# Attention and feed-forward layers on one core: where the split weights of a head group are kept and read in the first batch

## The reference, cut to what matters

```python
x = x + _L0_xattn_ref(4, 256, 256, w, u, _layernorm(x), ctx_2048)      # a recurrence over time
x = x + _L0_ffn_ref(_layernorm(x), kernel, bias)                       # an 8-bit feed-forward layer
x = x + _L1_xattn_ref(_layernorm(x), ctx_2048, ...)                    # attention: nearly all of the time
x = x + _L1_ffn_ref(_layernorm(x), ...)                                # a short linear-attention layer

def _L1_xattn_ref(hidden_states, cond, ...):        # 4 batches of 256 tokens of 256 channels
    q  = _ln(_fp8_linear_pertensor(ln_out, wq, wq_scale, q_in_scale)...)    # 16 heads of 128
    k  = _ln(_fp8_linear_pertensor(ln_out, wk, wk_scale, k_in_scale)...)    # 8 groups, 2 heads each
    v  = _fp8_linear_pertensor(ln_out, wv, wv_scale, v_in_scale)
    core = _gqa(q, k, v)
    qx = _ln(_fp8_linear_pertensor(ln_out, wqx, wqx_scale, qx_in_scale)...)
    kx, vx = split(einsum('bsi,oi->bso', cond, w_kv_x)); kx = _ln(kx)
    xout = _gqa(qx, kx, vx)
    catq = _div_clamp_fp8(concatenate([core, xout]), proj_smooth)
    return einsum('bsi,oi->bso', catq, wproj) * (proj_in_scale * proj_w_scale)
```

## Time and profile before

| | before |
|---|---|
| time, median of 3 runs | 708.38 us (707.12 to 709.31) |
| span of the profiled execution, first to last instruction | 708.0 us |
| PE busy | 623.2 us (88%) |
| DVE busy | 552.2 us (78%) |
| ACT busy | 421.1 us (59%) |
| POOL busy | 274.9 us (39%) |
| DMA, mean over the span | 113 GB/s, 80.09 MB |
| mean granted TensorE clock | 0.973 of full speed |

### The profile page before, as it was taken

One profiled execution on the slowest core, in us unless ns is written; L12 is line 12 of the kernel. 1 busy time (PEld: TensorE's weight loads), 2 busy tenths in 40 slices (PEclk: granted clock), 3 DMA queues, 4 the chain that ended last, 5 costly groups with the idle time before them and its releaser, 6 DMA issues.

```text
span 708.0 us, 13489 instructions
## 1 busy us (share of the span) xinstructions
PE 623.2 (88%) x4521; PEld 496.4 (70%) x4567; DVE 552.2 (78%) x1340; ACT 421.1 (59%) x1371; POOL 274.9 (39%) x371
## 2 busy tenths in 40 slices
PE   4347989988889999999999999999899999999946
PEld 3246767766668777777777877777788787786725
DVE  7997778976677857879788669888864677769698
ACT  4246766755677736566856556657665566673631
POOL 3224663442423563433335544333333256341131
PEclk9987999998999999999999999999999999999987
DMA  8255844743472222322234223422343233320001
GB/s 268 68 181 171 305 127 143 221 156 121 110 229 111 97 98 97 98 98 98 98 112 97 98 82 109 101 97 98 98 146 108 67 124 103 98 31 1 0 1 59
DMA packets 38414, 80.09 MB, mean 113 GB/s; under 512 B 3502, under 2 KB 28746, under 8 KB 33610
## 3 DMA queue, kind: packets, MB, share of 16 engines
q1 hardware_dynamic: 38160, 79.21, 35.5%
q10 hardware_dynamic: 186, 0.02, 0.0%
HBM read 66.62 MB, written 12.60 MB: 112 GB/s over the span
## 4 chain that ended last, share of the span: by engine, by line
PE 57%; DVE 27%; issue 5%; ACT 5%; POOL 3%; DMA 2%; SPq 0%; DVEq 0%; ACTq 0%; POOLq 0%
PE bank L588 12%; PE bank L712 12%; PE bank L692 9%; PE bank L595 6%; PE bank L661 4%; PE bank L736 3%; PE bank L678 2%; DVE Cb L1755 2%; DVE nm L1740 2%; POOL rs L1318 2%; PE bank L693 1%; PE bank L726 1%; DMA WH<-wh_split 1%; DVE Cb L1770 1%; DVE Cb L1771 1%
## 5 line engine op out<-in xcount | busy, mean ns | idle before, releaser
L712 PEld LDWEIGHTS bank<-V,Pt 128*128 128x128 f32 x1024 | 126.7, 192 | 39.3 <-DVE Cb L1755 26.8
L712 PE MATMUL bank<-V,Pt 128*128 128x129 f32 x1024 | 138.0, 278 | 10.5 <-DVE Cb L1755 8.9
L1066 ACT ACTIVATE square<-bank 128x128 bf16<-128x128 f32 x372 | 98.1, 276 | 74.8 <-PE bank L588 45.3
L692 PE MATMUL bank<-QT,KTt 128*128 128x512 f32 x256 | 132.7, 600 | 2.7 <-POOL diag L1342 2.4
L1049 ACT ACTIVATE Pt<-bank 128x512 f32<-128x512 f32 x128 | 76.6, 599 | 74.6 <-remote 49.4
L1740 DVE TENSOR_REDUCE nm<-bank 128x2 f32<-128x512 f32 x128 | 82.1, 683 | 35.8 <-PE bank L678 35.7
L1318 POOL TENSOR_TENSOR rs<-ve,mhalf 128x6 f32<-128x6 f32 x64 | 94.7, 1480 | 5.3
L1342 POOL TENSOR_TENSOR diag<-identb,nm 128x512 bf16<-128x512 bf16 x64 | 67.0, 1047 | 67.3 <-DVE nm L1740 67.2
L588 PE MATMUL bank<-WQ,xq 128*128 128x256 f32 x496 | 79.0, 304 | 9.5 <-DMA WH<-wh_split 3.4
L588 PEld LDWEIGHTS bank<-WQ,xq 128*128 128x128 f32 x496 | 67.0, 196 | 21.9 <-DVE nm L1740 12.0
L1755 DVE SCALAR_TENSOR_TENSOR Cb<-bank,ro,ism 128x128 bf16<-128x128 f32 x256 | 78.1, 347 | 4.5
(11 more groups left out here) (241 smaller groups left out, 1117.2 us busy)
## 6 DMA issues: line engine op xcount, KB each, us to landing
WQ<-wq_split SPq DMA_DIRECT2D x29, 1024.0 KB, 7.7
WH<-wh_split SPq DMA_DIRECT2D x29, 384.0 KB, 8.9
ism<-smooth_inverse SPq DMA_DIRECT2D x32, 256.0 KB, 6.4
wq_split<-stage SPq DMA_DIRECT2D x6, 1024.0 KB, 4.6
wst<-in_L_xattn_wproj SPq DMA_DIRECT2D x16, 256.0 KB, 3.8
wh_split<-stageh SPq DMA_DIRECT2D x6, 384.0 KB, 4.4
wst<-in_L_xattn_wq SPq DMA_DIRECT2D x8, 256.0 KB, 4.7
wst<-in_L_xattn_wqx SPq DMA_DIRECT2D x8, 256.0 KB, 4.7
```

What stands on the lines that cost most here:

```text
L692: nc.tensor.matmul(o[:], KTt[u % 2][:, x, t * P:(t + 1) * P], QT[u % 2][:, x, :], start=True, stop=False)
L712: last = nc.tensor.matmul(o[:, h * (P + 2):h * (P + 2) + P + 1], Pt[:, x, k, h * S + t * P:h * S + (t + 1) * P], V[u % 2][:, x, k, 0:P + 1 ...
L1066: last = A(square[:, t, h], head(t, h), ACT.Square, accum_out=ss[:, t, h:h + 1])
```

## The change

`stage` and `stageh` go. `WQ` and `WH` become rings of three buffers each, and group or unit `n` uses buffer `n % 3` for making, storing, loading and reading alike. The memory in bytes stays the same, since the two stage tiles had the size of one buffer.

- In batch 0 every unit reads its weights where they were made. `load_weights` is called for `u >= 8` only, 24 times. `weights_ready(u)` for `u < 8` waits for `wl_ready`, `wr_ready` and `wc_evac`.
- Making group `g >= 3` waits, on ACT ahead of its first write, until group `g - 3` is stored and unit `g - 3` has been projected. DVE's and POOL's own waits for stores go.
- Loads run three units ahead: `load_weights(8)` and `load_weights(9)` are both issued in loop 6, then `load_weights(u + 3)` in loop `u`. The wait of each, `qkv_done >= 4 * (u' - 2)` for load `u'`, is reached at the same point of loop `u` as that of `load_weights(u + 2)` was.

```diff
-        WQ = [eb(f"WQ{i}", [P, 2, KT, 4 * P], F32R) for i in range(2)]
-        WH = [eb(f"WH{i}", [P, 3, KT, 2 * P], BF16) for i in range(2)]
+        WQ = [eb(f"WQ{i}", [P, 2, KT, 4 * P], F32R) for i in range(RING)]
+        WH = [eb(f"WH{i}", [P, 3, KT, 2 * P], BF16) for i in range(RING)]
-        stage = eb("stage", [P, 2, KT, 4 * P], F32R)
-        stageh = eb("stageh", [P, 3, KT, 2 * P], BF16)
...
-            return (stage, stageh) if u == G - 1 else (WQ[u % 2], WH[u % 2])
+            return WQ[u % RING], WH[u % RING]
+        def stored_before(g):
+            return 32 * (g // RING)
+        def loads_before(u):
+            return 32 * ((u - G) // RING + 1)
...
             def load_weights(u):
-                g = u % G
-                sp.wait_ge(s["qkv_done"], 4 * (u - 1))
-                if u < G:
-                    sp.wait_ge(s["wq01_stored"], 64)
-                    sp.wait_ge(s["wq_stored"], 16 * (g - 1))
-                    sp.wait_ge(s["wh_stored"], 16 * (g - 1))
-                else:
-                    sp.wait_ge(s["wq_stored"], 16 * (G - 2))
-                    sp.wait_ge(s["wh_stored"], 16 * (G - 2))
+                g, i = u % G, u % RING
+                if u == G:
+                    for k in range(RING):
+                        sp.wait_ge(s[f"ring{k}_stored"], 32 * len(range(k, G, RING)))
+                sp.wait_ge(s["qkv_done"], 4 * (u - RING + 1))
...
                 if u == 0:
-                    load_weights(2)
                     store_thin(3)
-                    load_weights(3)
                     store_wide(4)
-                elif u != 1 and u + 2 != G - 1 and u + 2 < UNITS:
-                    load_weights(u + 2)
+                if u == G - 2:
+                    load_weights(G)
+                if u >= G - 2 and u + RING < UNITS:
+                    load_weights(u + RING)
...
             def weights_ready(u):
-                if u < 2 or u == G - 1:
+                if u < G:
                     pe.wait_ge(s["wl_ready"], 3 * (u + 1))
                     pe.wait_ge(s["wr_ready"], u + 1)
+                    pe.wait_ge(s["wc_evac"], u + 1)
                 else:
-                    pe.wait_ge(s[f"wq{u % 2}_loaded"], 32 * (u // 2 - (u % 2 if u >= G else 0)))
-                if u < G:
-                    pe.wait_ge(s["wc_evac"], u + 1)
+                    pe.wait_ge(s[f"ring{u % RING}_loaded"], loads_before(u))
...
             def weights(g, n, o=XB):                 # on ACT
-                    if g >= 3 and n in (0, 2):
-                        act.wait_ge(s["wh_stored" if n else "wq_stored"], 16 * (g - 2))
+                    if g >= RING and n == 0:
+                        act.wait_ge(s[f"ring{g % RING}_stored"], stored_before(g))
+                        act.wait_ge(s["qkv_done"], 4 * (g - RING + 1))
...
             def narrow_parts(g):                     # on POOL
-                if g >= 3:
-                    pool.wait_ge(s["wh_stored"], 16 * (g - 2))
...
             def low_weights(g, n, o=XB):             # on DVE
-                    if g >= 3 and n == 0:
-                        dve.wait_ge(s["wq_stored"], 16 * (g - 2))
```

More of the change, by code:

```diff
@@ L70, in build_program @@
     T8 = B * NT
+    RING = 3
     main = ExitStack()
@@ L241, in round_of @@
             return (ROUNDS[u][i],) if u < G else ()
-        def halves_of(g):
-            return (WQ[g], WH[g]) if g < 2 else (stage, stageh)
         def unit_weights(u):
-            return (stage, stageh) if u == G - 1 else (WQ[u % 2], WH[u % 2])
+            return WQ[u % RING], WH[u % RING]
[3 more added lines that the diff above has]
+            return 32 * ((u - G) // RING + 1)
         def out_weights(g):
@@ L280, in build_program @@
             "x_loaded x_rest_loaded ctx_loaded rows_loaded vecs_loaded kern_loaded bias_loaded smooth_loaded wst0_loaded "
-            "wst1_loaded wp0_loaded wp1_loaded ism0_loaded ism1_loaded w3_loaded wo_loaded rw_loaded smooth_stored wq_stored wh_stored wq01_stored "
-            "wq0_loaded wq1_loaded out_stored "
+            "wst1_loaded wp0_loaded wp1_loaded ism0_loaded ism1_loaded w3_loaded wo_loaded rw_loaded smooth_stored ring0_stored ring1_stored "
+            "ring2_stored ring0_loaded ring1_loaded ring2_loaded out_stored "
             "consts_ready rowsT_done vec_ready inv_ready insw_ready smooth_inverted kernT_done kscale_ready kdiag_ready "
@@ L353, in store_wide @@
                 sp.wait_ge(s["wl_ready"], 3 * (g + 1))
-                sp.dma_start(wq_dram[g], halves_of(g)[0][:].bitcast(F32).rearrange("p a k c -> p (a k c)")
-                             ).then_inc(s["wq_stored" if g >= 2 else "wq01_stored"], 16)
+                sp.dma_start(wq_dram[g], unit_weights(g)[0][:].bitcast(F32).rearrange("p a k c -> p (a k c)")
+                             ).then_inc(s[f"ring{g % RING}_stored"], 16)
             def store_thin(g):
                 sp.wait_ge(s["wr_ready"], g + 1)
-                sp.dma_start(wh_dram[g], halves_of(g)[1][:].rearrange("p a k c -> p (a k c)")
-                             ).then_inc(s["wh_stored" if g >= 2 else "wq01_stored"], 16)
+                sp.dma_start(wh_dram[g], unit_weights(g)[1][:].rearrange("p a k c -> p (a k c)")
+                             ).then_inc(s[f"ring{g % RING}_stored"], 16)
             def load_smooth(u):
@@ L371, in load_weights @@
             def load_weights(u):
-                g = u % G
-                sp.wait_ge(s["qkv_done"], 4 * (u - 1))
-                if u < G:
-                    sp.wait_ge(s["wq01_stored"], 64)
-                    sp.wait_ge(s["wq_stored"], 16 * (g - 1))
-                    sp.wait_ge(s["wh_stored"], 16 * (g - 1))
-                else:
-                    sp.wait_ge(s["wq_stored"], 16 * (G - 2))
-                    sp.wait_ge(s["wh_stored"], 16 * (G - 2))
-                sp.dma_start(WQ[u % 2][:].bitcast(F32).rearrange("p a k c -> p (a k c)"), wq_dram[g]
-                             ).then_inc(s[f"wq{u % 2}_loaded"], 16)
-                sp.dma_start(WH[u % 2][:].rearrange("p a k c -> p (a k c)"), wh_dram[g]).then_inc(s[f"wq{u % 2}_loaded"], 16)
+                g, i = u % G, u % RING
[3 more added lines that the diff above has]
+                sp.wait_ge(s["qkv_done"], 4 * (u - RING + 1))
+                sp.dma_start(WQ[i][:].bitcast(F32).rearrange("p a k c -> p (a k c)"), wq_dram[g]
+                             ).then_inc(s[f"ring{i}_loaded"], 16)
+                sp.dma_start(WH[i][:].rearrange("p a k c -> p (a k c)"), wh_dram[g]).then_inc(s[f"ring{i}_loaded"], 16)
             def load_weights3():
@@ L1020, in weights @@
                 x2 = o[:].rearrange("p (k c) -> p k c", k=KT)
-                wide, thin = halves_of(g)
+                wide, thin = unit_weights(g)
                 if n < 3:
@@ L1329, in narrow_parts @@
                 pool.wait_ge(s["wl_ready"], 3 * (g + 1))
-                if g >= 3:
-                    pool.wait_ge(s["wh_stored"], 16 * (g - 2))
-                thin = halves_of(g)[1]
+                thin = unit_weights(g)[1]
                 chain.add(gp.tensor_copy(thin[:, 1], rest[:]))
@@ L1688, in low_weights @@
                 if n < 3:
-                    (wide, thin), x2 = halves_of(g), o[:].rearrange("p (k c) -> p k c", k=KT)
+                    (wide, thin), x2 = unit_weights(g), o[:].rearrange("p (k c) -> p k c", k=KT)
                     dve.wait_ge(s["w_evac"], 8 * g + (2, 4, 8)[n])
```

## The result

| | before | after |
|---|---|---|
| time, median | 707.95 us (4 runs, 707.12 to 709.31) | 703.20 us (4 runs, 702.33 to 704.45) |
| the same, measured again | 708.10 us (18 runs, 705.30 to 710.65) | 703.46 us (7 runs, 701.24 to 704.46) |
| ratio, 95% interval | | 0.9941 [0.9917, 0.9965]; again 0.9931 [0.9905, 0.9957] |
| span of the profiled execution | 708.0 us | 700.6 us |
| DMA bytes | 80.09 MB | 72.87 MB |

The kernel is 4.7 us faster (4.6 in the second measurement), and the forecast of 702.6 us is met within 0.6 us (0.9 in the second). The ratio is an estimate of its own from the runs, not the quotient of the two medians, which is 0.9933. The profiled execution of after took 702.40 us for its span of 700.6, so 1.8 us lie outside a span. That was not known ahead.

The account below looks back on a forecast made before the run. The chain lay 57% on TensorE and 27% on DVE, with one load waited for, group 6's. Span 708.0 less 5.8 is 702.2, plus 0.4 gives 702.6 us; own range 701.5 to 704.8, 8 in 10 within 700.2 to 705.6.

Parts of the forecast that it names:

- The wait itself: TensorE's wait for group 6's reload before `project(6, 0)` goes, so that starts at 162.39 instead of 166.03: 3.64 us.
- The clock behind the wait: From 166.03 to 171.44 TensorE ran at granted clock 0.50 because of the wait; full clock returns 2.55 us.
- the wait alone, if the clock falls all the same: Lower bound of the saving around `project(6, 0)`: 3.6 us, with the slow clock behind it remaining.
- 0.4 us by which the median stands above the span: Added to the forecast span of 702.2 us to give the forecast median of 702.6 us.
- What is late next: DVE's `maxima(5, 1, 0)` behind the guard starts at 166.38 instead of 172.18, limiting the gain to 5.80 us.
- the place of the tiles: Wide matmuls reading from the ring buffers instead of the stage: 0, with 0.5 us either way as bound.
- the spare unit: From loop 7 on each load is needed a unit later; none was waited for, so it gains 0.
- A: Rival: a DVE wait of about 2.6 us replaces TensorE's DMA wait in batch 0; 705.6 to 708 us, chance 0.10.
- B: Rival: the wait at 99.12 and its clock fall in batch 0 go too, 5 us more; 697.5 us, chance 0.07.
- C: Rival: no gain, as POOL's step of group 6 is the true bound or the making moved; 708.4 us, chance 0.04.
- D: Rival: the doubled load at the batch change delays `project(8, 0)`, losing 8.2 us; 710.8 us, chance 0.05.
- The rule that was weighed: Skill rule that DVE copying from PSUM keeps TensorE warm; prediction held that idle time lowers the clock, whoever ends it.

Follow-up runs that it names:

- e1_narrow6: Kernel before with only POOL's step of group 6 moved ahead of the second reciprocal root, stage and 29 loads kept: 703.23 us, ratio 0.9931.
- e2_reload6: Changed kernel with group 6 loaded back from DRAM over its ring buffer and unit 6 waiting for that load: 708.68 us, ratio 1.0015.
- e5_warm_wait: Kernel before with 30 unread bf16 matmuls on TensorE ahead of its wait for the load of group 6: 706.02 us, ratio 0.9977.
- e4_traffic: Changed kernel with five loads of 1024 KB into an unread tile put back into batch 0: 702.55 us, ratio 0.9932.
- e3_two_ahead: Changed kernel with loads for batches 1 to 3 issued two units ahead instead of three: 703.26 us, ratio 0.9931.
- e0_after: The changed kernel itself, unaltered, measured again beside the kernel before on one chip: 703.46 us against 708.10, ratio 0.9931.
- e6_fill_start: Changed kernel with three idle stretches of TensorE ahead of the first unit filled with unread matmuls: 702.09 us, ratio 0.9921.
- e8_fill_two: Changed kernel with three fillings ahead of the first unit and a fourth in TensorE's wait for DVE in loop 1: 701.27 us, ratio 0.9903.

## Why the prediction was right

- *Where the time was.* Right: one load of 29. `e1_narrow6` removes that wait alone and has all of the gain; `e2_reload6` brings it alone back and has none.
- *The wait itself.* The forecast put `project(6, 0)` 0.92 us behind the `weigh`, and that is what it took. The wait itself, which the forecast put at 3.64 us, is the part that every execution pays; with no fall of the clock the saving was 3.3 us.
- *The clock behind the wait.* The mechanism was right (`e5_warm_wait`), the size was that of one execution. The term "2.55 us more" is 0 to 2.4 us: 10.86 - 8.47 = 2.4 in the profile that the sum used, 9.71 - 8.47 = 1.2 in another, 0 in a third. The prediction had "the wait alone, if the clock falls all the same" as its lower bound, 3.6; it should have had "if the clock does not always fall", and its middle, 4.7, is what the medians show. That the forecast came so near is in part luck: one profile could not tell how often the clock falls.
- *Where the sum started.* The term "0.4 us by which the median stands above the span" set a time against a span. By the 1.8 us outside a span, the median of 708.38 belongs to a span of some 706.6 (an estimate), 1.4 less than the 708.0 of the profile. The sum comes out all the same, because it is the median less 5.8.
- *What is late next.* DVE went into its maxima with no wait, and the stretch shortened by 5.73 us against 5.80.
- *The four other loads, their traffic, the added wait, the place of the tiles, the spare unit.* Each was counted 0. The traffic and the spare unit are 0 as far as `e4_traffic` and `e3_two_ahead` can tell, ACT's waits are unchanged, and all together cost the 0.3 us of 465.05 against 465.32, within the 0.5 allowed for the place of the tiles. The sign "batches 1 to 3 are as long as before" came true but for that.
- *The rivals.* A did not happen: TensorE's next wait for DVE was the 0.28 us in front of `project(6, 1)`. (Its price has a slip: 708.4 less 3.2 and less 0.7 is 705.2 to 707.7, not 705.6 to 708. The forecast's own range also takes the 0.5 us of places off its lower end, 701.4, and does not add it to its upper, 705.3. Neither decides anything here.) B looked right in the first pair of traces, whose spans differ by 7.4 us, but 1.9 of that come from the clock ahead of the wait, which differs between executions of either kernel: `e0_after` gave 1.3 of them back (162.03 against 160.75), `e3_two_ahead` all. C did not happen: both intervals of the ratio lie below 1. D was tested and is nothing: the first pair of loads landed as before.
- *An idle time that was misread.* The prediction has TensorE idle 1.7 us inside 157 to 163. That wait ended at 157.92, so 0.9 us of it lie inside; the 1.4 us missing from 4.60 of 6.00 are these and the start of the stall. That the clock was still 1.00 in 157 to 163 is right.
- *The rule that was weighed.* TensorE's wait for DVE in loop 1 lowers the clock in nine of the twelve profiles where it is not filled, and costs 1.1 us when it does: from the first `diag` of unit 1 to that of unit 2, `e6_fill_start` takes 21.81 us, and after, where the clock stayed up behind the same wait of 2.60 us, 20.67 (`e8_fill_two`, which fills it, 20.66). The row that the prediction set against the rule is borne out. By these traces the sketch of the Trainium skill, "TensorE: Matmul & The Clock Gate", section "Loop structure matters more than you think", in which a copy out of PSUM by DVE does no harm and the next matmuls follow immediately, holds only while TensorE has such work during the copy.

## What to carry to other kernels

A load that is hidden 28 times of 29 is worth looking at for the one time: find the wait, and see what finished last ahead of it. Here a buffer scheme over three engines and the loads of a batch did what moving one POOL step by one place does.

A stall of TensorE has two prices, its length and the slow clock behind it, and the second differs between executions of the same kernel. Take it from several profiles, and compare medians and not two spans. Here the medians saw about half of the full price (4.6 - 3.3 of 2.4 us).

## What the runs showed of the hardware

- Matmuls whose result nobody reads, put into a wait of 3.4 us, saved 2.2 us of a kernel by the medians (0.5 to 2.8 by the interval). Put into a wait of 13.3 us at whose end DVE was busy 98% of the time they saved nothing.
- After the same wait of 3.3 to 3.4 us the granted clock over the next six us was 0.50, 0.72 or 1.00 in three executions of one program. In the second of them it fell after TensorE had begun to work again.
- A wait of 2.6 us, ended by DVE, left the granted clock of 98 to 104 us at 0.72 in nine profiles and at 1.00 in three.
- Two loads of 1408 KB issued back to back: the first kept its 5.0 and 5.5 us, the wide half of the second took 8.1.
